# One cast per chunk for the adjacency masks of a relational graph layer, on ScalarE for every fourth chunk and on GpSimd for the others

## What is computed

```
h   = relu(layernorm(x))                       # per node, over the features
P   = h @ W_loop.T
G   = P @ Wg_loop.T
v   = (P + b_loop) * sigmoid(G + bg_loop)      # messages, [m, d]
out = x + relu(sum over m of (adj[m, n] == 1) * v[m])
```

## Time and profile before

| | us |
|---|---|
| median of 3 runs | 104.6 |
| the 3 runs | 104.58, 104.6, 105.48 |
| the profiled execution, device time | 104.03 |
| its span | 102.2 |
| busy: TensorE / VectorE / ScalarE / GpSimd | 95.4 / 90.1 / 88.6 / 85.8 |

### The profile page before, as it was taken

One profiled execution on the slowest core, in us unless ns is written; L12 is line 12 of the kernel. 1 busy time (PEld: TensorE's weight loads), 2 busy tenths in 40 slices (PEclk: granted clock), 3 DMA queues, 4 the chain that ended last, 5 costly groups with the idle time before them and its releaser, 6 DMA issues.

```text
span 102.2 us, 2493 instructions
## 1 busy us (share of the span) xinstructions
PE 95.4 (93%) x802; PEld 91.3 (89%) x802; DVE 90.1 (88%) x196; ACT 88.6 (87%) x144; POOL 85.8 (84%) x162
## 2 busy tenths in 40 slices
PE   5986899998999999999999999999999999999960
PEld 2655789797999999999999999999999999999950
DVE  2289989999999999999999999999999788777761
ACT  5075498899799998999899989998999989898990
POOL 2188999999999999999999999999999999991000
PEclk9999999999999999999999999999999999999996
DMA  1899999999999999999999999999945150606345
GB/s 50 242 319 292 290 290 290 291 293 294 293 312 298 328 328 331 311 329 322 333 282 317 271 324 316 327 292 313 345 134 157 58 151 28 184 6 205 103 140 168
DMA packets 50288, 25.45 MB, mean 249 GB/s; under 512 B 866, under 2 KB 50276, under 8 KB 50276
## 3 DMA queue, kind: packets, MB, share of 16 engines
q1 hardware_dynamic: 50000, 25.17, 88.5%
q10 hardware_dynamic: 276, 0.13, 0.4%
HBM read 16.91 MB, written 8.39 MB: 247 GB/s over the span
## 4 chain that ended last, share of the span: by engine, by line
PE 71%; POOL 4%; ACT 3%; issue 1%; DVE 0%; POOLq 0%
PE psum L786 23%; PE psum L764 12%; PE psum L769 12%; PE psum L765 12%; PE psum L751 11%; POOL rstd L339 3%; ACT junk L442 2%; POOL xn L352 1%; ACT gate L436 0%; PE psum L811 0%; DVE dist_sum L628 0%; DVE flag L630 0%; POOLq L362 0%
## 5 line engine op out<-in xcount | busy, mean ns | idle before, releaser
L352 POOL TENSOR_SCALAR xn<-x_all,mean_neg,rstd 128x128 f32<-128x128 f32 x101 | 44.7, 454 | 0.7 <-POOL rstd L339 0.4
L764 PE MATMUL psum<-w_hi,hT_hi 128*128 128x256 f32 x128 | 33.8, 299 | 1.3 <-DVE w_lo L589 0.9
L786 PE MATMUL psum<-vals,mask 128*128 128x128 f32 x256 | 33.6, 275 | 0.1
L421 ACT ACTIVATE psum<-bias_all 128x1024 f32<-128x1024 f32 x32 | 33.1, 1035 | 0.3 <-DVE vals L557 0.3
L786 PEld LDWEIGHTS psum<-vals,mask 128*128 128x128 f32 x256 | 31.0, 191 | 0.2 <-issue 0.2
L765 PE MATMUL psum<-w_lo,hT_hi 128*128 128x256 f32 x128 | 31.0, 277 | 0.0
L524 DVE BATCH_NORM_STATS2 stats<-x_all 128x6 f32<-128x256 f32 x64 | 23.9, 418 | 3.2 <-DMA x_all<-in_x 3.0
L764 PEld LDWEIGHTS psum<-w_hi,hT_hi 128*128 128x128 f32 x128 | 24.1, 188 | 2.0 <-DVE w_lo L589 1.1
L557 DVE TENSOR_TENSOR vals<-psum,gate 128x512 f32<-128x512 f32 (+1 forms) x33 | 21.9, 663 | 3.9 <-ACT gate L436 3.3
L339 POOL TENSOR_TENSOR rstd<-var_eps,minus_half 128x16 f32<-128x16 f32 (+2 forms) x11 | 24.5, 2225 | 0.1
L765 PEld LDWEIGHTS psum<-w_lo,hT_hi 128*128 128x128 f32 x128 | 24.2, 189 | 0.0
(11 more groups left out here) (36 smaller groups left out, 31.3 us busy)
## 6 DMA issues: line engine op xcount, KB each, us to landing
adj_all<-in_adj SPq DMA_DIRECT2D x16, 512.0 KB, 6.8
x_all<-in_x SPq DMA_DIRECT2D x15, 512.0 KB, 6.8
out<-x_all SPq DMA_DIRECT2D x14, 512.0 KB, 6.2
out<-x_all SPq DMA_DIRECT2D x3, 256.0 KB, 2.3
x_all<-in_x SPq DMA_DIRECT2D x2, 256.0 KB, 3.0
out<-x_all ACTq DMA_DIRECT2D x1, 128.0 KB, 2.5
out<-x_all SPq DMA_DIRECT2D x1, 128.0 KB, 2.6
w_raw<-in_L_gnn_W_loop SPq DMA_DIRECT2D x1, 64.0 KB, 2.5
```

What stands on the lines that cost most here:

```text
L352: last = pool.tensor_scalar(xn[:, g % XN, j * D:j * D + D], x_all[:, g * GC + j * D:g * GC + j * D + D], mean_neg[:, b % BATCH_SLOTS, k:k ...
L421: nc.scalar.activation(prod_ps[s].rearrange("p g a d -> p g (a d)"), bias_all[:, :, :].rearrange("p a d -> p (a d)").unsqueeze(1) .to_broa ...
L764: nc.tensor.matmul(to, hi, w_hi[:, :], start=False, stop=False, skip_group_check=True)
L786: last = nc.tensor.matmul(to[:, j * D:j * D + D], mask[:, g % MASKS, j * N:j * N + N], vals[:, s, j * D:j * D + D], start=True, stop=True)
```

## The change

Groups 0 to 3 keep one cast each, on ScalarE. From group 4 on, one instruction casts both groups of a chunk, 128x1024 instead of twice 128x512, issued at the place where the cast of the chunk's even group stands; the odd group has none. It waits for the aggregation that frees the second of its two slots, one group later than the wait of the even group's cast before, and counts two on the semaphore. ScalarE has the chunks of groups 8, 16 and 24, GpSimd the other eleven (4, 6, 10, 12, 14, 18, 20, 22, 26, 28, 30). By groups ScalarE has ten casts' worth as before (0 to 3, 8, 9, 16, 17, 24, 25) and GpSimd 22; groups 4, 12 and 20 go from ScalarE to GpSimd, and 9, 17 and 25 from GpSimd to ScalarE.

```diff
+        def mask_width(g):
+
+            return 1 if g < MASKS else 0 if g % CHUNK else CHUNK
+
         def mask_by_act(g):
-            return g < 4 or g % MASKS == 0 and g < LAST_MASK_ACT
+            return g < MASKS or g // CHUNK % 4 == 0 and g < LAST_MASK_ACT
...
                 pool.wait_ge(adj_loaded[g // CHUNK], 16)
-                if g >= MASKS:
-                    pool.wait_ge(summed, g - (MASKS - 1))
-                pool.tensor_copy(mask[:, g % MASKS, :], adj_all[:, g * GC:g * GC + GC]
-                                 ).then_inc(mask_ready, 1)
+                w = mask_width(g)
+
+                pool.wait_ge(summed, g + w - MASKS)
+                pool.tensor_copy(mask[:, g % MASKS:g % MASKS + w, :].rearrange("p s m -> p (s m)"),
+                                 adj_all[:, g * GC:(g + w) * GC]).then_inc(mask_ready, w)
...
-                if live(t + 1) and not mask_by_act(t + 1):
+                if live(t + 1) and mask_width(t + 1) and not mask_by_act(t + 1):
                     edges(t + 1)
...
                 act.wait_ge(adj_loaded[g // CHUNK], 16)
+                w = mask_width(g)
                 if g >= MASKS:
-                    act.wait_ge(summed, g - (MASKS - 1))
-                nc.scalar.activation(mask[:, g % MASKS, :], adj_all[:, g * GC:g * GC + GC], ACT.Copy
-                                     ).then_inc(mask_act, 1)
+                    act.wait_ge(summed, g + w - MASKS)
+                nc.scalar.activation(mask[:, g % MASKS:g % MASKS + w, :].rearrange("p s m -> p (s m)"),
+                                     adj_all[:, g * GC:(g + w) * GC], ACT.Copy).then_inc(mask_act, w)
...
-                if live(t + 2) and mask_by_act(t + 2):
+                if live(t + 2) and mask_width(t + 2) and mask_by_act(t + 2):
                     edges(t + 2)
```

## The result

| | before | after |
|---|---|---|
| median of 12 runs | 104.61 us | 105.43 us |
| lowest and highest | 104.11, 105.48 | 105.06, 105.73 |
| profiled execution, its span | 104.03, 102.2 | 105.55, 103.8 |
| start of the turn of group 6 to that of group 31 | 67.86 us | 68.88 us |

The account below looks back on a forecast made before the run. GpSimd and TensorE were taken to bound the steady part together. A loss of 0.35 us from the late start plus 0.05 for waits made 0.40: 104.6 + 0.4 = 105.0 us, range 104.2 to 106.1.

Parts of the forecast that it names:

- What bounds: In the steady part GpSimd and TensorE bound together, within 0.02 us per four groups, tightest at each batch's first group.
- The price of the double cast: One GpSimd cast for two groups takes 1049 ns, 1.03 us from start to start.
- the rival without a saving: On GpSimd a double cast saves nothing and takes 1.20 us; 106.3 us in all, chance 0.12.
- The place behind the rstd: On GpSimd the first graph begins 3.07 us after rstd without a cast between; a cast there costs only 0.39 us.
- The start: Up to group 10 GpSimd has two double casts, 2.06 us against 1.57; group 10 is turned 0.43 us late.
- The later batches: Groups 14 and 22 in time, 18 and 26 waiting for GpSimd about 0.1 us each; the loss stays at 0.35.
- the bursts: ScalarE's work from the cast of group 16 to the end of group 18's bias, 5.11 us, and its like elsewhere.
- What trails a wait: A wait costs TensorE a little more than its length; 0.05 us added for up to five places.
- "I cost it at nothing": ScalarE's double cast, 0.41 to 0.54 us more, is hidden by 0.54 us between group 18's bias and its products.
- The rival: ScalarE's burst makes TensorE wait for the bias of groups 10, 18 and 26: 0.9 us more, 105.9 us, chance 0.12.
- The port pair: Rival: each of 11 GpSimd casts holds VectorE up by up to 0.44 us more; 106.2 us, chance 0.02.

Follow-up runs that it names:

- three of the runs: The changed kernel with ScalarE's chunks in single casts (106.39 us), with groups 4 and 5 cast singly as before (105.61 us), and with both edits (106.06 us).
- the start was undone: The changed kernel with group 4 cast by ScalarE and group 5 by GpSimd in single casts where they stood before: 105.61 us, ratio 1.0100.
- without the three watches: The changed kernel without ScalarE's watch (sums for the check) in steps 7, 15 and 23: 104.60 us, ratio 1.0008.
- with the start as before as well: The changed kernel without ScalarE's watch in steps 7, 15 and 23, and groups 4 and 5 cast singly on ScalarE and GpSimd: 104.25 us, ratio 0.9973.

## Why the prediction was right in kind and half in size

- *What bounds.* Right that TensorE and GpSimd ran together at the first group of each batch: a little less on GpSimd removed every irregular distance behind group 8 and gave 0.4%. Incomplete in that ScalarE was as close (0.39 us of spare time at the bias of group 18), and VectorE too, whose graph of group 14 made that turn late in three of the runs.
- *The price of the double cast.* Right: 1.049 us forecast, 1.046 measured. (The price from which the rival without a saving decides comes out of its sum at 1.11 us, not 1.13: 0.40 + 8 x 0.08 = 1.04.)
- *The place behind the rstd.* Right: 3.07 forecast, 3.06 measured. The sum for eight groups was 21.67; from the coefficients of group 10 (31.45) to those of group 18 (52.97) it is 21.52, and to those of group 26 (74.40) another 21.43. The error of 0.15 is at least in part in the graphs: ten in a row take 4.32 us from start to start (34.98 to 39.30), 0.432 each, where I had 0.443.
- *The start.* Right: from turn 6 to turn 10 11.24 us against 10.93, 0.31 late where 0.43 was forecast, and gone when the start was undone.
- *The later batches.* Wrong for this kernel. Groups 18 and 26 don't wait for GpSimd. By the sum TensorE was to wait 0.1 us at each; the 0.15 and 0.24 of the two stretches of eight groups and the other losses of TensorE put GpSimd's graphs 0.98 us ahead at 26. Where the bursts are taken away, a wait of about this size does show, once in each kernel: 2.78 at group 18 without the three watches, 2.84 at group 26 with the start as before as well. The bursts hid it.
- *What trails a wait.* Undersized. I put 0.05 us on it for all places. Behind group 10 the next three distances are 2.80, 2.75, 2.74, 0.22 us together. The same row, 7 behind 6, was in the trace before and I took only its first distance. Why TensorE is slower behind a wait stays open; no run was aimed at it.
- *"I cost it at nothing".* This is the step that failed. For ScalarE's double cast I had 0.54 us of distance from bias to product, 0.43 more work, and added 0.33 because TensorE would be late itself. The work measured is 55.71 to 56.66, 0.95 against 0.54, so 0.41 more: right. Three things were not. The handover of the bias, 0.15 us, was not taken off the 0.54, so that 0.39 were spare and not 0.54. Being late gave nothing back, because ScalarE's own stretch begins from a turn of TensorE (in both traces its `hT_hi` of group 15 begins 0.63 us behind that turn) and is late by as much. And ScalarE entered the burst later, its `hT_hi` of group 16 1.04 us behind the turn (53.81 and 52.77) where it was 0.94 (52.84 and 51.90). 0.39 - 0.41 - 0.10 is -0.12, where the product came 0.17 late. At group 26 the same sum has 1.26 us behind the turn instead of 0.94: 0.39 - 0.41 - 0.32 is -0.34, and the product came 0.33 late. Most of this 0.32 came over VectorE: the bias of group 23 at 73.50 had waited 0.20 us for VectorE's `vals` and began 0.80 us behind its `hT_hi`, 0.49 before, where no bias behind group 6 waits for VectorE. The rival named the place (bias of groups 18 and 26) and had 0.12 of the chance; it, beside the start, is what happened, smaller than its 0.9. That the time stayed within 1% is in part luck: one wait too many, for GpSimd at 18 and 26, stood in the sum where ScalarE's was missing.
- *The port pair.* Given 0.02, and true in mechanism: a graph of VectorE is kept out by a cast. I read 27 graphs between 326 and 405 ns as a test of it, but in the trace before only two of them had begun inside a cast (28.59 and 88.68), 0.09 and 0.27 us before its end, and the test could see next to nothing. In the changed kernel it has little weight by luck of timing: the graph at 68.42 took 0.70 us beside the cast that began at 68.01 and was done 0.12 us ahead of its turn, and the one of group 14 began 0.14 us ahead of the cast. In the three runs in which that graph met the cast TensorE was 0.15 to 0.47 us late there. In the run without bursts it can't be told from nothing.

The Trainium skill (SBUF — State Buffer, section Who interferes with whom) has VectorE in a two-port mode and GpSimd exclude one another for a whole instruction. The casts of these runs agree (1.15 and 1.05 us beside 1.04); GpSimd's 128x128 graphs, which read SBUF as well, do not (VectorE at 0.26 us a graph, GpSimd at 0.50), and there the measurement decides.

## What to carry to other kernels

When four engines each work 97% of the time or more in lockstep, ask of every wider instruction what stands between the same two handovers on its engine: its length there counts, not the average load, and doing it where that engine already has its long steps is the wrong place. Delays on different engines hide one another, and an edit that takes one away shifts all engines by some tenths of a us and can bring up a third: here single casts on ScalarE and the better start each let VectorE's graph meet a cast. So undo them together before calling one harmless, and in every variant read anew which engine is late at each long distance; the place alone doesn't say. And a row that "never shows" an interference is evidence only if the two instructions did overlap in time; count the overlaps first.

## What the runs showed of the hardware that I had not expected

- TensorE's first product begins 0.14 to 0.15 us behind the end of ScalarE's bias in every long distance at 20 and 28 here, and a turn that waits for VectorE's graph begins 0.10 us behind its end (47.57 and 47.67).
- Two casts of GpSimd one behind the other keep VectorE's float32 graph out over both: 1.29 us beside 1.16 us of casts, against 0.33 alone.
- GpSimd's own normalisations beside VectorE's go 0.50 us each instead of 0.44, and VectorE isn't slowed.
- A wait of TensorE of 0.1 to 0.5 us for `xn` is followed by a distance of 2.79 to 2.84 us and one or two of about 2.75 instead of 2.69, at a granted clock of 1.00 (36.40 to 44.69 of the change), in every kernel here; behind the waits for ScalarE's bias it was sometimes absent (28: 3.02, then 2.70).
